# A state-space, attention and expert block on one core: joint projection of an order's two directions, a third of a convolution on VectorE, the value bias outside TensorE, routing of the last image by halves

## The chip, the cores and the metric

The kernel runs on one core of a Trainium2 chip. The metric is the device time of one execution in microseconds (us), a median of several runs. A core has TensorE (PE, matrix products; PEld is its weight load), VectorE (DVE), ScalarE (ACT), GpSimd (POOL) and SyncE (SP), which here only issues DMAs. Each engine runs its own instructions in their written order, and semaphores order the engines among each other.

## What is computed

Four images of 32x32 pixels with 384 channels pass three residual layers. Shortened from the reference:

```python
x = x + L0(_gn(x))                       # state-space layer, 4 scans
t = _to_tokens(x)                        # 4096 tokens of 384
t = t + L1_attn(_ln_t(t))                # linear attention, 12 heads
t = t + L1_ffn(_ln_t(t))                 # 8 experts, top 1, capacity 512

# L0
xz = x @ in_proj_w.T
xh, z = jnp.split(xz, 2, axis=-1)        # 192 channels each
xc = silu(depthwise_conv3x3(xh) + conv_b)
xs = [by rows, by columns, by rows flipped, by columns flipped]      # K = 4
x_dbl = jnp.einsum('bkdl,kcd->bkcl', xs, x_proj_w)
dts, Bs, Cs = jnp.split(x_dbl, [R, R + N], axis=2)                   # R = 24, N = 16
dts = softplus(jnp.einsum('bkrl,kdr->bkdl', dts, dt_projs_w) + dt_projs_b)
out_y = selective_scan(xs, dts, -exp(A_logs), Bs, Cs, Ds)
y = norm(sum of the four orders) * silu(z);  return y @ out_proj_w.T

# L1_attn, without softmax
attn = jnp.einsum('bhnd,bhmd->bhnm', q, k) / sqrt(32)
out = jnp.einsum('bhnm,bhmd->bhnd', attn, v);  return out @ w_proj + b_proj

# L1_ffn
expert_gate, expert_index = max and argmax of softmax(xf @ router_w)
position_in_expert = running count of the tokens of that expert      # dropped from 512 on
h = gelu(expert_inputs @ w1 + b1);  y = gelu(h @ w2 + b2);  out = gate * y
```

## The kernel before

**Layout.** All of it is one program with six stages; every SBUF tile is a view of one tensor, `arena`, and every PSUM tile a view of `ps`, so the profile's rows are told apart by their lines. Two images lie above each other on the 128 partitions (a pair, `p` = 0 or 1), each with 64 of the 192 channels, so the channels make J = 3 thirds of a pair. A direction `k` = 0 to 3 is an order `o = k % 2` (rows, columns) and a sense `dr = k // 2` (forward, flipped). An order's two directions have the same input.

**Prologue (0 to 258 us).** Group norm, input projection `in_proj` (L1048), the 3x3 convolution and the preparation of the scans. Pair 0's convolution and the first third of pair 1's are nine taps each on VectorE (`taps` L1486, `first_third` L1498 and L1502). The second and third thirds of pair 1 are on PE: seven taps as products with diagonal matrices (`conv`, 14 matmuls a third in two calls, L1060), the last two on VectorE (`last_taps`, L1517). The order is written out by tables: `FILL_ORDER` gives the two PSUM slots in turn, `CONV_AT` the half after whose `delta_product` a call of `conv` stands, `LAST_TAPS_AT` the same for VectorE, `SILU_AT` the step at which ScalarE applies silu to pair 1.

After the convolution each pair has HALVES = 12 halves: direction `k` by third `j`, `(k, j) = divmod(i, J)`. For each direction `x_proj(p, k)` (6 matmuls, L1076) puts the time-step rows on PSUM partitions 0 to 47 and the rows of B and C on 64 to 127. ScalarE copies them out (`split_hi`: L713 for the rows that later work reads, L714 for the bf16 high part); VectorE subtracts that (`split_rest`, L1530), ScalarE casts the middle part (`split_mid`, L718), VectorE subtracts again (`split_lo`, L1534). So B and C are kept as three bf16 parts that the scans' PE products add up. SP stores them in HBM (`store_parts`). Each half then takes these steps, and each engine runs them one half after another:

- PE: `delta_product` (2 matmuls, L1088); the line shows 4 instructions, as fp32 matmuls count twice in the trace.
- ScalarE: `dt_out` (absolute value L729, plain copy L730), `exp_abs` (L735), for even halves `one_more` (1 + u, L744), and for the half before `log_w` (L749).
- VectorE: for odd halves 1 + u itself (L1546), then `lost_part` (L1549), and for the half before `finish` (L1556, L1559, L1563).
- SP: `store_delta`, two stores a half. The buffers of a half turn over MADE = 4 places, those of 1 + u over 2, which is why a step waits for `pd_ok` of two halves before.

GpSimd copies pair 1's convolved thirds into column order (`by_columns`, L552) in between.

**Scans (258 to 1414 us).** 12 tiles of 32 units on PE, ScalarE, VectorE (L1628, L1645) and GpSimd (L564, L581). The change doesn't touch them.

**Norm, gate, output projection (1414 to 1504 us), then attention (1504 to 1708 us).** Per image: `mirror`, `keys` (one row of sums L1302, then L1307), `values` (L1316 and, for the bias of the values, one matmul a third with one row of contraction, L1318), `mixed` (L1325), `bias_row` (L1331), `weights` (L1345), `attend` for eight tiles (L1356), with the next image's `turn_and_gram` (L1279 to L1287) put in between. VectorE takes `keys`, `values` and `bias_row` out of PSUM (L1771, L1775, L1781, L1788) and adds the result to the tokens (`attended`, L1795, L1796).

**Routing.** Per image VectorE runs `stats`, `rsqrt`, `normalise`, `logits`, `choose`, `place` (L1802 to L1873), with an exp on ScalarE and two small products on PE (`cumsum`, L1337, L1338) between. GpSimd then scatters the image's 8 tiles of tokens to their slots in HBM (`scatter`, L619). Images 0 to 2 do this during the next image's attention. For image 3 nothing follows: all eight tiles are attended, then routed, then scattered; SP loads the second weights of expert 0 (L511) as soon as the slots are known, and after the last scatter the slots of expert 0 (L514) and the weights of expert 1 (L516, L517). **Experts (1741 to 2258 us):** `turn_slots` (L1393), then w1 (L1404) and w2 (L1416); an expert starts when both of its weights are in.

## Time and profile before

| | |
|---|---|
| median of 3 runs | 2261.23 us (2260.4 to 2262.72) |
| the profiled execution, its own time | 2259.55 us |
| its span in the trace | 2257.7 us |
| busy: PE / VectorE / GpSimd / ScalarE | 88% / 70% / 58% / 51% |
| TensorE clock granted, mean | 0.971 |

The span is what the trace covers, and 1.85 us of the execution lie around it. A page of the profile gives the busy share of each engine in 40 slices, the chain of waits that ended last, and the instructions in groups by line. Busy shares are means over stages with different limits, so each stage is read on its own. In a row, "[5.15 <-ACT arena L744]" means that the engine stood idle for 5.15 us before it, and that the instruction of line 744 on ScalarE ended this.

### The profile page before, as it was taken

The page shows a single profiled execution, that of the slowest core. Times are in us where ns is not written, and L with a number is a line of the kernel's source. Part 1 is how long each engine was busy: PE and PEld are TensorE (multiplying, and loading weights), DVE is VectorE, ACT ScalarE, POOL GpSimd, SP SyncE. Part 2 cuts the span into 40 slices and gives each one's busy share as a digit, 9 for nine tenths or more (in the row PEclk, how much of TensorE's full clock was granted, in tenths as well). Part 3 has the DMA queues.
Part 4 walks back from the last instruction along what each step waited for, and adds up shares of the span by engine and source line. Part 5 has one row for each costly group of instructions (what it writes and reads, how often), then busy time and mean ns, then how long its engine had stood idle before and what let it go on. Part 6 is the DMA issues. An engine that isn't in the chain of part 4 may idle for free.

```text
span 2257.7 us, 20191 instructions
## 1 busy us (share of the span) xinstructions
PE 1996.3 (88%) x5862; PEld 923.9 (41%) x5862; DVE 1579.7 (70%) x1480; ACT 1150.4 (51%) x1249; POOL 1299.1 (58%) x464
## 2 busy tenths in 40 slices
PE   7998588888888888888888888989994999999997
PEld 3433133333333333333333333456652555555554
DVE  6899999999999999999999999753553000000000
ACT  4789676767666676766666776211221121111111
POOL 0110399999999999999999999401333011111110
PEclk9996599999999999999999999999997999999999
DMA  5447622133222233222232220511226133333300
GB/s 187 178 162 265 209 75 75 57 107 83 78 70 65 74 102 88 65 74 74 71 96 70 79 65 19 228 42 56 84 85 237 64 121 124 124 119 125 126 24 7
DMA packets 79346, 228.84 MB, mean 101 GB/s; under 512 B 10895, under 2 KB 37121, under 8 KB 77760
## 3 DMA queue, kind: packets, MB, share of 16 engines
q1 hardware_dynamic: 73152, 211.25, 29.1%
q0 software_dynamic: 6144, 16.98, 2.1%
q8 instruction: 24, 0.39, 0.1%
q14 instruction: 26, 0.21, 0.0%
HBM read 166.10 MB, written 64.03 MB: 102 GB/s over the span
## 4 chain that ended last, share of the span: by engine, by line
PE 44%; DVE 26%; issue 17%; POOL 9%; ACT 3%; DMA 1%; DVEq 0%; ACTq 0%; POOLq 0%; SPq 0%
DVE arena L1645 15%; PE ps L1404 11%; PE ps L1416 11%; PE ps L1147 6%; POOL arena L581 5%; POOL arena L564 4%; PE ps L1356 3%; PE ps L1131 2%; DVE arena L1486 2%; DVE ps L1628 1%; PE ps L1144 1%; PE ps L1307 1%; PE ps L1048 1%; PE ps L1345 1%; DVE arena L1556 1%
## 5 line engine op out<-in xcount | busy, mean ns | idle before, releaser
L581 POOL TENSOR_TENSOR arena<-arena 128x2048 f32<-128x2048 f32 x192 | 871.3, 4551 | 17.6 <-DVE arena L1645 16.6
L1147 PE MATMUL ps<-arena 128*128 128x512 f32 x1536 | 726.5, 595 | 29.0 <-POOL arena L581 28.9
L1645 DVE TENSOR_TENSOR_SCAN arena<-arena,ps 128x1024 f32<-128x1024 f32 x264 | 588.9, 2276 | 0.0
L844 ACT ACTIVATE arena<-ps 128x1024 f32<-128x1024 f32 x384 | 390.7, 1017 | 249.0 <-PE ps L1131 247.1
L1131 PE MATMUL ps<-arena 96*128 (+1 forms) x1296 | 366.6, 384 | 128.1 <-DVE arena L1645 112.9
L1147 PEld LDWEIGHTS ps<-arena 128*128 128x128 f32 x1536 | 287.8, 189 | 288.6 <-issue 192.9
L564 POOL TENSOR_TENSOR arena<-arena 128x1024 f32<-128x1024 f32 x120 | 283.9, 2366 | 94.3 <-DMA arena<-b_rows 94.3
L1943 DVE TENSOR_TENSOR arena<-ps,arena 128x384 f32<-128x384 f32 x32 | 17.8, 558 | 449.7 <-PE ps L1416 449.7
L1628 DVE TENSOR_TENSOR ps<-ps,arena 128x1024 f32<-128x1024 f32 x264 | 310.1, 1223 | 13.2 <-PE ps L1131 13.2
L837 ACT ACTIVATE arena<-arena 128x1024 f32<-128x1024 f32 x264 | 300.7, 1139 | 9.0 <-DVE arena L1645 8.6
L1131 PEld LDWEIGHTS ps<-arena 96*128 96x128 bf16 x1296 | 112.8, 98 | 460.2 <-DVE arena L1645 216.3
L641 POOL DMA_INDIRECT out<-arena x32 | 31.7, 992 | 436.6 <-DVE arena L1948 436.6
L1645 DVE TENSOR_TENSOR_SCAN arena<-ps,arena 128x1024 f32<-128x1024 f32 x120 | 272.8, 2273 | 4.6 <-ACT ps L837 4.2
L1416 PE MATMUL ps<-arena 128*128 128x384 f32 x768 | 250.2, 486 | 0.0
L1404 PE MATMUL ps<-arena 128*128 128x512 f32 x576 | 249.5, 594 | 0.0
L1416 PEld LDWEIGHTS ps<-arena 128*128 128x128 f32 x768 | 145.4, 190 | 101.6 <-issue 3.8
L837 ACT ACTIVATE ps<-arena 128x1024 f32<-128x1024 f32 x120 | 134.1, 1118 | 87.5 <-DVE arena L1645 87.5
L1404 PEld LDWEIGHTS ps<-arena 128*128 128x128 f32 x576 | 109.9, 191 | 136.3 <-issue 134.0
L981 ACT ACTIVATE arena<-ps,arena 128x512 f32<-128x512 f32 x96 | 66.0, 688 | 176.0 <-PE ps L1404 175.9
L614 POOL TENSOR_TENSOR arena<-arena 128x384 f32<-128x384 f32 x32 | 27.0, 874 | 190.7 <-DVE arena L1788 190.7
L988 ACT ACTIVATE arena<-arena 128x384 f32<-128x384 f32 x32 | 16.7, 523 | 232.3 <-DVE arena L1943 232.3
L552 POOL COPY arena<-arena 128x1024 f32<-128x1024 f32 x6 | 14.6, 2454 | 145.7 <-ACT arena L702 145.7
(211 smaller groups left out, 1632.6 us busy)
## 6 DMA issues: line engine op xcount, KB each, us to landing
arena<-b_rows SPq DMA_DIRECT2D x240, 256.0 KB, 4.2
arena<-in_w SPq DMA_DIRECT2D x16, 2304.0 KB, 16.3
delta<-arena SPq DMA_DIRECT2D x24, 512.0 KB, 2.7
delta_x<-arena SPq DMA_DIRECT2D x24, 512.0 KB, 2.7
arena<-delta SPq DMA_DIRECT2D x24, 512.0 KB, 3.6
arena<-delta_x SPq DMA_DIRECT2D x24, 512.0 KB, 4.6
slot_in<-arena SPq DMA_DIRECT2D x8, 772.0 KB, 8.1
arena<-slot_in SPq DMA_DIRECT2D x8, 772.0 KB, 18.0
```

Source lines behind the costliest of these rows:

```text
L564: nc.gpsimd.tensor_tensor(xin[:, x % XRING], xin[:, x % XRING], dux[:, dr], ALU.mult).then_inc(in_ok, 1)
L581: nc.gpsimd.tensor_tensor(hst[:, h:h + 2], hst[:, h:h + 2], c_sb[:, c:c + 2], ALU.mult).then_inc(p2_ok, 2)
L837: nc.scalar.activation(dst, dlt[:, dr], ACT.Exp, scale=a_neg[:, q % OJ, dr, n:n + 1]).then_inc(dec_ok, 1)
L844: nc.scalar.activation(c_sb[:, u % RING], C_PS, ACT.Copy).then_inc(c_free, 1)
L981: nc.scalar.activation(h_sb[:, m], ps[:, 3 + m % 3, :], ACT.Gelu_apprx_tanh, bias=b1_col[:, e, m:m + 1]).then_inc(hg_ok, 1)
L1131: mm = pe.matmul(dst[:, h * 512:(h + 1) * 512], sel_lhs[0:BR, n], bc[0:BR, q % OJ // J, dr, m, h * 512:(h + 1) * 512], start=True, stop=True)
L1147: mm = pe.matmul(Y_PS[:, h * 512:(h + 1) * 512], ident, hst[:, u % HRING, h * 512:(h + 1) * 512], start=False, stop=(u == UN - 1))
L1356: mm = pe.matmul(ps[:, attend_bank(i), 0:CA], xnT[:, b % 2, t, i * P:(i + 1) * P], w_eff[:, t], start=(t == 0), stop=(t == CT - 1))
L1404: mm = pe.matmul(ps[:, 3 + m % 3, :], w1[s][:, t, m * P:(m + 1) * P], xeT[:, s, t], start=(t == 0), stop=(t == CT - 1))
L1416: mm = pe.matmul(ps[:, 6 + i % 2, 0:C], h_sb[:, m, i * P:(i + 1) * P], w2[s][:, m], start=(m == 0), stop=(m == MT - 1))
L1628: nc.vector.tensor_tensor(x, x, dux[:, dr], ALU.mult).then_inc(p1_ok, 1)
L1645: nc.vector.tensor_tensor_scan(h, f, x, 0.0, ALU.mult, ALU.add).then_inc(sc_ok, 1)
```

## The change

It has five parts.

1. **Joint projection.** `x_proj` is now called for an order: once for the time-step rows of both directions ("xd", 64 partitions each) and once for B and C of both ("xa"), 6 matmuls each, so 8 calls in all as before. ScalarE copies the time-step rows (`dt_rows_out`); for "xa" it copies the rows (`split_hi`, first) and casts the high part from all 128 partitions (second). PE subtracts the high part inside PSUM with `minus` (a negated identity in bf16, `take_hi`), ScalarE casts the middle part (`split_mid`), PE subtracts it (`take_mid`), ScalarE casts the low part (`split_lo`). VectorE has no part in it. The four directions come in the order `K_ORDER` = 0, 2, 1, 3. The weights of the projection are loaded by four DMAs in pieces of 64 floats, the weights `dt_w` a second time for the partitions from 64 on.
2. **Convolution.** VectorE convolves the second third of pair 1 as well, with nine taps; PE keeps the third one. VectorE makes 1 + u for two halves of three (`i % J`) instead of one of two, ScalarE for the other.
3. **Bias of the values.** The three products with one row are gone. `keys` puts its row of sums on all 128 partitions; VectorE scales it by the bias as a column (`bv_col`) and adds it before the mask.
4. **Routing of the last image by halves.** Four tiles each (`ROUTED`): statistics per tile as it is attended, the first half's slots and scatter before the second half's. ScalarE normalises the last image's tokens (two ACTIVATEs a tile) and takes the inverse root as exp(-0.5 ln).
5. **Expert 0's second weights** have a semaphore of their own, are loaded after the slots, and PE waits for them between w1 and w2.

```diff
+ROUTED = [(b, 0, TB) for b in range(B - 1)] + [(B - 1, 0, TB // 2), (B - 1, TB // 2, TB)]
...
-FILL_ORDER.insert(len(IN_ORDER) - 1, ("x", 0, 0))
-FILL_ORDER += [("x", 0, 1), ("conv", 1, 1), ("x", 0, 2), ("x", 0, 3), ("conv", 1, 2)]
-FILL_ORDER += [("x", 1, k) for k in range(K)]
+FILL_ORDER.insert(len(IN_ORDER) - 1, ("xd", 0, 0))
+FILL_ORDER += [("xa", 0, 0), ("xd", 0, 1), ("conv", 1, 2), ("xa", 0, 1)]
+FILL_ORDER += [("xd", 1, 0), ("xa", 1, 0), ("xd", 1, 1), ("xa", 1, 1)]
...
-CONV_AT = {1: (1, 0), 4: (1, 1), 7: (2, 0), 8: (2, 1)}
-LAST_TAPS_AT = {4: 1, 8: 2}
-SILU_AT, NEXT_PAIR_AT = HALVES - 3, HALVES - 2
+CONV_AT = {3: 0, 4: 1}
+LAST_TAPS_AT = 5
+SILU_AT = 6
+DT_ROWS_AT = {(0, 2): (0, 1), (0, 8): (1, 0), (1, 1): (1, 1)}
+BC_ROWS_AT = {(0, 0): (0, 0), (0, 5): (0, 1), (0, 10): (1, 0), (1, 3): (1, 1)}
+HI_AT = {(0, 0): (0, 0), (0, 6): (0, 1), (1, 0): (1, 0), (1, 4): (1, 1)}
+K_ORDER = (0, 2, 1, 3)
...
+            for k in range(K):
+                o, dr = k % 2, k // 2
+                sp.dma_start(xproj_w[:, o, :, :, H2 * dr:H2 * dr + H2],
+                             a["xproj_w"][:, k].rearrange("p j (s c) -> p j s c", s=2)).then_inc(ld_c, 16)
...
-            sp.wait_ge(idx_ok, B)
-            sp.dma_start(w2[0], w2_v[0]).then_inc(ld_w[0], 16)
+            sp.wait_ge(idx_ok, B + 1)
             sp.wait_ge(scat, 16 * NT)
             slot_in_v = slot_in.rearrange("(e i p) c -> e p i c", i=CPT, p=P)
             sp.dma_start(xe, slot_in_v[0]).then_inc(ld_xe, 16)
+            sp.dma_start(w2[0], w2_v[0]).then_inc(ld_w2[0], 16)
...
+                nc.scalar.activation(b_full[0:H2 + SR], slot[0:H2 + SR], ACT.Copy).then_inc(hi_ok, 1)
+                nc.scalar.activation(parts[:, o, 0], slot, ACT.Copy).then_inc(hi_ok, 1)
+
+            def split_mid(p, o):
+                act.wait_ge(less_ok, 2 * (p * 2 + o) + 1)
+                nc.scalar.activation(parts[:, o, 1], fill_slot("xa", p, o), ACT.Copy).then_inc(mid_ok, 1)
...
                     if s < HALVES:
                         dt_out(p, s)
                         exp_abs(p, s)
-                        if s % 2 == 0:
+                        if s % J == 0:
                             one_more(p, s)
                     if s >= 1:
                         log_w(p, s - 1)
...
+                    if (p, s) in HI_AT:
+                        split_hi(*HI_AT[p, s])
+                    if (p, s - 1) in HI_AT:
+                        split_mid(*HI_AT[p, s - 1])
+                    if (p, s - 2) in HI_AT:
+                        split_lo(*HI_AT[p, s - 2])
+                    if (p, s - 1) in DT_ROWS_AT:
+                        dt_rows_out(*DT_ROWS_AT[p, s - 1])
...
+            def take_part(p, o, part):
+
+                for h in range(2):
+                    mm = pe.matmul(fill_slot("xa", p, o)[:, h * 512:(h + 1) * 512], minus, parts[:, o, part, h * 512:(h + 1) * 512],
+                                   start=False, stop=True, skip_group_check=True)
+                return mm
...
                     if s + 1 < HALVES:
                         delta_product(p, s + 1)
...
+                    if (p, s - 2) in HI_AT:
+                        take_mid(*HI_AT[p, s - 2])
                     if p == 0 and s in CONV_AT:
...
+                    if (p, s - 1) in HI_AT:
+                        take_hi(*HI_AT[p, s - 1])
+                    if (p, s) in BC_ROWS_AT:
+                        x_proj("xa", *BC_ROWS_AT[p, s])
+                    if (p, s) in DT_ROWS_AT:
+                        x_proj("xd", *DT_ROWS_AT[p, s])
...
-                    mm = pe.matmul(ps[:, VK_PS, t * P:(t + 1) * P], bkv[0:1, 1, t * P:(t + 1) * P], w_row[0:1, t * P:(t + 1) * P],
-                                   start=False, stop=True, skip_group_check=True)
...
+            chain.link(nc.vector.tensor_tensor(by_block, bv_rows, ident.unsqueeze(1).to_broadcast([P, CT, P]), ALU.mult))
+            chain.link(nc.vector.tensor_reduce(bv_col, by_block, AX.X, ALU.add))
...
-                nc.vector.tensor_tensor(bd.rearrange("p t c -> p (t c)"), ps[:, VK_PS, 0:C], head_mask, ALU.mult).then_inc(bd_ok, 1)
+                if b:
+                    dve.wait_ge(m_ok, b * CT)
+                flat = bd.rearrange("p t c -> p (t c)")
+                chain.link(nc.vector.tensor_tensor(flat, ps[:, VK_PS, 0:C], w_row, ALU.add))
+                nc.vector.tensor_tensor(flat, flat, head_mask, ALU.mult).then_inc(bd_ok, 1)
...
+            for i in range(1, 4):
+                attended(b, i)
+                tile_stats(b, i - 1)
+            tile_stats(b, 3)
+            last_means(0)
+            attended(b, 4)
+            tile_stats(b, 4)
+            logits(b)
+            attended(b, 5)
+            choose(b)
+            attended(b, 6)
+            tile_stats(b, 5)
+            gates(b)
+            attended(b, 7)
+            tile_stats(b, 6)
+            tile_stats(b, 7)
+            last_means(1)
+            place(b)
+            logits(b + 1)
+            choose(b + 1)
+            gates(b + 1)
+            place(b + 1)
```

How the tables move PE's work in the middle of pair 0 is seen best in its instructions. Before, from the second call of `conv` (L1060) on, with `delta_product` (L1088) and `x_proj` (L1076) between:

```order
L1060 MATMUL ps<-arena 128x512 x7
L1088 MATMUL ps<-arena 128x512 x4
L1076 MATMUL ps<-arena 128x512 x6
L1088 MATMUL ps<-arena 128x512 x2
L1060 MATMUL ps<-arena 128x512 x7
L1088 MATMUL ps<-arena 128x512 x2
L1060 MATMUL ps<-arena 128x512 x7
```

and now the same stretch, `conv` on L1123, `delta_product` on L1167, `x_proj` on L1139, the subtraction of a part on L1147:

```order
L1147 MATMUL ps<-arena 128x512 x2
L1139 MATMUL ps<-arena 128x512 x6
L1167 MATMUL ps<-arena 128x512 x2
L1123 MATMUL ps<-arena 128x512 x7
L1167 MATMUL ps<-arena 128x512 x2
L1123 MATMUL ps<-arena 128x512 x7
L1167 MATMUL ps<-arena 128x512 x2
L1139 MATMUL ps<-arena 128x512 x6
```

Two calls of `conv` are gone. The other two stand directly behind an "xd" projection and ahead of an "xa" projection, with one `delta_product` between each (those of halves 4, 5 and 6).

ScalarE now, at half 6 of pair 0 (`dt_out` L767 and L768, `exp_abs` L773, `one_more` L782, `log_w` L787, `split_hi` L747 and L748, silu L729):

```order
L773 ACTIVATE arena<-arena 128x1024
L782 ACTIVATE arena<-arena 128x1024
L787 ACTIVATE arena<-arena 128x1024
L747 ACTIVATE arena<-ps 96x1024
L748 ACTIVATE arena<-ps 128x1024
L843 ACT_TABLE_LOAD
L729 ACTIVATE arena<-arena 128x1024 x3
L846 ACT_TABLE_LOAD
L767 ACTIVATE arena<-ps,arena 128x1024
```

The silu stood at step 9, between two halves and with no copies ahead of it; it is at step 6 now, right behind a `one_more` and the two copies of a `split_hi`.

VectorE at the end of the last image's routing, from the last `attended` on (before, everything from the statistics to `place` stood behind it):

```order
L1871 TENSOR_TENSOR arena<-arena,ps 128x384
L1895 BN_STATS arena<-arena 128x6 x2
L1902 BN_AGGR arena<-arena 128x2 x4
L1904 TENSOR_SCALAR arena<-arena 128x4
L1956 TENSOR_TENSOR arena<-ps,arena 128x32
...
L1976 TENSOR_TENSOR arena<-arena 128x4
L1919 TENSOR_TENSOR arena<-arena 128x4
...
L1936 TENSOR_TENSOR arena<-arena 128x32
L1942 TENSOR_REDUCE arena<-arena 128x4
...
L1976 TENSOR_TENSOR arena<-arena 128x4
```

Behind the last tile now come `place` of the first half (L1956 to L1976, which releases its scatter), then `logits`, `choose`, `gates` and `place` of the second half; the first half's `logits`, `choose` and `gates` have moved ahead, between the tiles.

## Rows read from the trace of the kernel before

**Rows 1.** By stage: length; busy PE, PEld, DVE, ACT, POOL; PE clock; DMA; GB/s.

```profile
92.00:158.00 66.00, 64.44 (x141) 25.73 (x140) 57.47 (x50) 60.01 (x59) 0.00 (x0) 0.97 0.45 160
158.00:258.00 100.00, 70.36 (x109) 25.01 (x107) 96.38 (x82) 84.85 (x85) 7.26 (x3) 0.64 0.63 224
...
1708.00:1741.00 33.00, 4.17 (x18) 3.73 (x18) 12.06 (x51) 3.03 (x5) 9.13 (x10) 0.56 0.76 265
```

**Rows 2.** VectorE in time order, 80 to 258 us: start, duration, idle before.

```profile
101.47 1.23 DVE L1549 SCALAR_TENSOR_TENSOR arena<-arena 128x1024 f32<-128x1024 f32 x1 [5.15 <-ACT arena L744]
...
160.94 2.83 DVE L1549 SCALAR_TENSOR_TENSOR arena<-arena 128x1024 f32<-128x1024 f32 x1
...
202.23 1.23 DVE L1549 SCALAR_TENSOR_TENSOR arena<-arena 128x1024 f32<-128x1024 f32 x1
...
207.03 1.22 DVE L1549 SCALAR_TENSOR_TENSOR arena<-arena 128x1024 f32<-128x1024 f32 x1
```

**Rows 3.** VectorE by line, 80 to 258 us: busy, mean ns, idle before.

```profile
L1502 DVE SCALAR_TENSOR_TENSOR arena<-arena 128x1024 f32<-128x1024 f32 x8 | 11.9, 1487 | 0.3
L1530 DVE TENSOR_TENSOR arena<-ps,arena 64x1024 f32<-64x1024 f32 x8 | 9.8, 1228 | 0.2
L1534 DVE TENSOR_TENSOR arena<-arena 64x1024 bf16<-64x1024 f32 x8 | 9.8, 1222 | 0.3
L1546 DVE TENSOR_SCALAR arena<-arena 128x1024 f32<-128x1024 f32 x12 | 9.1, 757 | 1.9 <-ACT arena L735 1.7
L1517 DVE SCALAR_TENSOR_TENSOR ps<-arena,ps 128x1024 f32<-128x1024 f32 x2 | 2.6, 1290 | 0.1
```

**Rows 4.** ScalarE in time order: the same step of two halves in a row.

```profile
113.60 1.11 ACT L729 ACTIVATE arena<-ps,arena 128x1024 f32<-128x1024 f32 x1
...
117.50 1.11 ACT L729 ACTIVATE arena<-ps,arena 128x1024 f32<-128x1024 f32 x1
```

**Rows 5.** ScalarE by line, 92 to 258 us: a table load.

```profile
L803 ACT ACT_TABLE_LOAD x1 | 1.3, 1283 | 0.0
```

**Rows 6.** PE in time order, prologue: products and their time at either clock.

```profile
96.35 5.42 PE L1076 MATMUL ps<-arena 128*128 128x512 f32 x12
...
103.61 6.28 PE L1060 MATMUL ps<-arena 128*128 128x512 f32 x14
109.81 3.70 PE L1088 MATMUL ps<-arena 48*128 48x512 f32 x8
...
173.73 7.19 PE L1088 MATMUL ps<-arena 48*128 48x512 f32 x8 [7.82 <-ACT arena L713]
180.85 8.09 PE L1076 MATMUL ps<-arena 128*128 128x512 f32 x12
```

**Rows 7.** DMA traffic from 20 to 22 us.

```profile
DMA packets 1177, 0.60 MB, mean 298 GB/s; under 512 B 760, under 2 KB 1142, under 8 KB 1155
```

**Rows 8.** PE in time order, `values` and `mixed` of image 3.

```profile
1676.11 0.48 PE L1318 MATMUL ps<-arena 1*128 1x128 f32 x2
1676.53 0.94 PE L1316 MATMUL ps<-arena 128*128 128x128 f32 x6
...
1679.81 2.24 PE L1325 MATMUL ps<-arena 128*128 128x392 f32 x6 [0.65 <-DVE arena L1781]
```

**Rows 9.** VectorE in time order, image 3's last tile and routing.

```profile
1708.41 0.55 DVE L1796 TENSOR_TENSOR arena<-arena,ps 128x384 f32<-128x384 f32 x1
...
1717.46 0.22 DVE L1850 TENSOR_TENSOR arena<-ps,arena 128x64 f32<-128x64 f32 x1
...
1721.08 0.17 DVE L1873 TENSOR_TENSOR arena<-arena 128x8 uint32<-128x8 f32 x1
```

**Rows 10.** GpSimd in time order, the first of image 3's eight scatters.

```profile
1722.05 0.97 POOL L619 DMA_INDIRECT slot_in<-arena  x1 [16.77 <-DVE arena L1873]
```

**Rows 11.** The chain that ended last, from the last scatter on.

```profile
1730.99 2.49 DMA slot_in<-arena
1733.50 4.59 DMA arena<-slot_in
```

More of the change, by code:

```diff
@@ L429, in _ @@
             for p in range(NP):
-                store_parts(p, 0)
                 if p == 0:
@@ L628, in _ @@
             scatter(B - 1)
+            scatter(B)
             def residuals(e, s):
@@ L1835, in choose, with tile_stats, last_means @@
-            def choose(b):
-                tb = slice(b * TB, (b + 1) * TB)
+            def tile_stats(b, i):
+                dve.wait_ge(ta2_ok, 1 + b * TB + (i + 1))
+                ins = nc.vector.bn_stats(bst5[:, i], tok[:, b * TB + i, :])
+                if i % 4 == 3:
+                    chain.link(ins)
+            def last_means(g):
+                settled(dve)
+                for i in range(4 * g, 4 * g + 4):
+                    ins = nc.vector.bn_aggr(mv5[:, i], bst5[:, i])
+                chain.link(ins)
+                nc.vector.tensor_scalar(neg_mean[:, 4 * g:4 * g + 4], mv5[:, 4 * g:4 * g + 4, 0], -1.0, None, ALU.mult).then_inc(tvar_ok, 1)
```

414 lines of the change are left out of this document (228 added, 186 removed).

## Prediction

> **What bounds the kernel now.** I first split the span by stage [rows 1], since the change touches three stages and leaves the scans and the experts alone.
>
> From 158 to 258 us VectorE is busy for 96.4 of 100 us, ScalarE for 84.9, PE for 70.4 at a granted clock of 0.64. So VectorE sets the end of the prologue, and ScalarE is close behind. From 92 to 158 us it is less clear: VectorE 57.5 of 66, ScalarE 60.0, PE 64.4 at full clock. In time order [rows 2] VectorE has one large hole, 5.15 us before its first `lost_part` at 101.47, where it waits for ScalarE. Later two halves in a row start 4.80 us apart (202.23 and 207.03): that is VectorE's price of a half without 1 + u. ScalarE's is 3.90 us (113.60 to 117.50, [rows 4]), one of its `one_more` or copies adds 1.0 to 1.1.
>
> Image 3's routing (1708 to 1741 us) is a stretch in which PE works for 4.2 of 33 us [rows 1]: a plain chain of VectorE, GpSimd and DMA. Attention before it is PE's.
>
> **The change, part by part.**
>
> *Prologue, VectorE's sum.* L1530 and L1534 go: 16 instructions of 1.23 us, 1.26 with the gap [rows 3], -20.1 us. Two last taps of 1.29 go, -2.6. L1546 grows from 12 to 16, 4 x 0.73 = +2.9. The third on VectorE is one TENSOR_SCALAR of 0.76 and eight taps of 1.3 (the mean of 1.49 in [rows 3] holds one that GpSimd's copy slowed), +11.2. Sum -8.6 us. But 11.2 - 2.5 of this lies before 101.47, where there is a hole of 5.15: VectorE comes to its first `lost_part` at 105.0, 3.5 later. From there on it has 17.3 us less to do. If VectorE stayed the only bound, the prologue would end 13.8 us earlier.
>
> *Prologue, what is late next.* It won't stay so. I lay the three engines' instructions in their new order, each as long as in the rows, each behind what it waits for. The same laying out of the old order gives the three holes of before up to 0.3 us and the end up to 2.2. Four places open:
>
> - Start: ScalarE's two copies of `split_hi` wait for "xa", which PE ends at 92.8 + 2 x 1.8 + 5.3 = 101.7 [rows 6]. Half 1's exp ends at 107; VectorE waits 0.9 us.
> - Halves 5 to 7, the largest. PE's `take_mid` waits for ScalarE until 109, behind it the "xd" projection ends at 115.2, `delta_product` 117.0, `conv` 6.2 (125.0 with the next product), `conv` again, product of half 6 at 133.0. ScalarE wanted it at 129.0. From 133.1 it has half 6 with `one_more` and the log of half 5 (5.3), the two copies (2.1), two table loads of 1.28 [rows 5] with three silus of 1.1 between (5.9), half 7 up to its exp (3.0): 149.4. VectorE is done at 142.4: a hole of 7.1 us, after one of 0.7. Before, the silu stood at half 9, where VectorE was behind and had no hole.
> - Second pair: 1.9 us behind the copies of "xa" (1, 0), 3.9 us at half 15, where ScalarE's `split_lo` waits 2.8 for `take_mid`, which stands behind an "xd" projection at half clock; 0.7 us at half 18.
>
> New holes 15.2 us, old ones after 101.47 some 2.3 in that laying out, so +13. Against it: GpSimd's three column copies slow VectorE's instructions that run beside them (2.83 us for one that takes 1.23 otherwise, [rows 2]), and they now fall mostly into the hole of 7.1 us, -3. Sum: +3.5 - 17.3 + 13 - 3 = **-4 us**, bounds -14 (all holes covered) and +2 (each of them half as long again). I take -4.5 for the term, since the trace has a further hole of 1.5 us at 195 that the laid out order hasn't.
>
> *PE in the prologue.* Eight projections stay. `conv` loses 14 matmuls of 6.28 in two calls, 12.6 us; eight pairs of bf16 products come, under 1 us a pair. PE isn't the bound except in the place above.
>
> *The weights of the projection.* They arrive in 3072 pieces of 256 bytes. In 2 us at 20 to 22 us the queues moved 760 packets under 512 bytes beside others [rows 7]: 3072 are 8.1 us, behind traffic that ends at 28. VectorE first asks for them at 38.5, so I cost this at nothing; bounds 0 and +4 (landing at 43 instead of 36). 
>
> *Attention.* L1318 goes: three per image, 0.42 us from its start to the next one's [rows 8], 12 in all, -5.1. PE has no hole there, so it counts in full. The second instruction of `values_out` (about 0.5) hides behind `turn_and_gram` (2 us) for images 0 to 2; for image 3 PE waits 0.65 for it [rows 8], so +0.6. `keys` loads 128 columns of weights instead of one, +0.1 an image. The column of the bias (two instructions of 0.5, before the tokens of tile 4 are normed, where PE waits for VectorE) +1.0. Sum **-3.1**, bounds -4.5 and -1.
>
> *Routing of image 3.* Before: last tile added at 1708.96, slots at 1721.25, eight scatters 1.28 apart from 1722.05 to 1730.99 [rows 9, 10], landing 2.5, slots in 4.6 [rows 11]. Now VectorE ends that tile at some 1709.5 (statistics between the tiles), two tiles' statistics 1.0, means 0.6, `place` of the first half 2.7 (L1850 to L1873 took 3.8 with the gates, [rows 9]), so its four scatters run from 1714.7 to 1719.8 beside VectorE's second half: logits 1.4, choose 1.1, gates 0.6, the cumulative sum's way over PE 0.7, place 2.7, slots at 1720.3. That is only 1 us earlier than before, but four scatters are left, not eight: 4 x 1.28 = 5.1. Sum **-6.0**. ScalarE's 16 ACTIVATEs of some 0.5 us and its two inverse roots end before the slots do. Bounds -8 (the slots' load, no longer behind 2.3 MB of weights) and -2 (ScalarE's tokens late).
>
> *Expert 0's weights.* They are asked for some 6 us later than before, behind the slots, and needed only after the expert's 36 products with w1, which take most of half an expert: nothing.
>
> **Sum:** -4.5 - 3.1 - 6.0 = -13.6 us. The profiled execution took 2259.55 us; on its own time that is 2246.0, against the median, which is 1.7 higher, **2247.6 us**.
>
> **The rivals.**
>
> *VectorE stays the bound in the prologue.* For it: it was the busiest for 100 us, and it starts pair 0 with work in hand. Against: ScalarE has 24 x 3.9 [rows 4] + 8 x 1.1 for `one_more` + 19 copies of 1.03 + 5.9 for silu = 128 us of work for the same 24 halves, so hardly any slack. -14 in place of -4.5: 2238.
>
> *The halves bring little.* If the last image's tokens, normalised on ScalarE, or the exp behind them come late, the second scatter starts late. Against it: 8 us of ScalarE work have 11 us. -2 in place of -6: 2251.6.
>
> *Slower: PE at half clock on the path.* PE has less to do and waits for ScalarE's casts in its own order. After 7.82 us of waiting the clock was at half and a projection took 8.09 us for 5.42 [rows 6]. If all eight projections lay on the path at that clock, 8 x 2.7 = 21.5 us come: 2269. It decides from five of eight on (13.6 / 2.7). Against it: only one or two have somebody waiting behind them.
>
> *The change does what it says* in all of its parts, as the listed instructions show; a part that adds nothing is in the range.
>
> **How the numbers follow.** The forecast 0.68, VectorE as the only bound 0.13, little from the halves 0.12, the slower case 0.04, several terms at their small ends together 0.03. The range reaches from a prologue of -11 to terms of -1.5, -1.5 and -4: **2240 to 2254**. A measurement of this kernel tells 0.2%, 4.5 us, from no change. Faster by more than that 0.93, same 0.03, slower 0.04.
>
> **What would show it.** VectorE's last `finish` near 253 instead of 257.7 us, with a hole of about 7 us in it near 145, ended by ScalarE. No instruction between 75 and 258 us on VectorE on 64 partitions. An attention image 1.2 us shorter. Four scatters from about 10 us before the other four, slots loaded some 6 us earlier after the last tile. It would be wrong if VectorE showed no hole in the prologue (gain too small), if PE stood at half clock with ScalarE waiting for it in most halves (too large), or if the last scatter came as long after the last tile as before.

## The result, and the profile after

| | before | after |
|---|---|---|
| median of the first runs (4 each) | 2261.47 us (2260.4 to 2262.72) | 2245.59 us (2243.82 to 2246.91) |
| the profiled execution, its span | 2259.55, 2257.7 us | 2246.46, 2244.7 us |
| ratio of the runs, 95% interval | | 0.9929 (0.9912 to 0.9946) |
| TensorE clock granted, mean | 0.971 | 0.968 |

The change makes the kernel 15.9 us faster; 2247.6 was forecast. The two profiled executions differ by only 13.0 us of span. The other 2.7 us lie in the profile of before that was taken first (the second one, below, shows it).

VectorE of the changed kernel in the prologue, and ScalarE beside it in the middle of pair 0, in order of time:

```profile
103.99 1.22 DVE L1621 SCALAR_TENSOR_TENSOR arena<-arena 128x1024 f32<-128x1024 f32 x1
107.45 0.69 DVE L1618 TENSOR_SCALAR arena<-arena 128x1024 f32<-128x1024 f32 x1 [2.25 <-ACT arena L773]
...
131.97 0.69 DVE L1618 TENSOR_SCALAR arena<-arena 128x1024 f32<-128x1024 f32 x1 [2.51 <-ACT arena L773]
...
153.21 0.69 DVE L1618 TENSOR_SCALAR arena<-arena 128x1024 f32<-128x1024 f32 x1 [7.07 <-ACT arena L773]
...
200.00 1.22 DVE L1621 SCALAR_TENSOR_TENSOR arena<-arena 128x1024 f32<-128x1024 f32 x1 [2.14 <-ACT arena L782]
...
253.46 2.36 DVE L1688 TENSOR_TENSOR ps<-ps,arena 128x1024 f32<-128x1024 f32 x2
```

```profile
128.87 1.11 ACT L767 ACTIVATE arena<-ps,arena 128x1024 f32<-128x1024 f32 x1 [4.11 <-PE ps L1167]
...
136.99 1.11 ACT L767 ACTIVATE arena<-ps,arena 128x1024 f32<-128x1024 f32 x1 [4.11 <-PE ps L1167]
...
144.28 1.28 ACT L843 ACT_TABLE_LOAD   x1
145.58 3.23 ACT L729 ACTIVATE arena<-arena 128x1024 f32<-128x1024 f32 x3
148.82 1.28 ACT L846 ACT_TABLE_LOAD   x1
```

The first `lost_part` (L1621) starts at 103.99 us, 2.5 later than before [rows 2], the scans (L1688) at 253.46, 4.3 earlier than the 257.75 of before. Between these two, VectorE before and after (columns as in [rows 1]):

```profile
101.47:257.75 156.28, 125.33 (x227) 47.12 (x226) 149.38 (x127) 136.35 (x135) 7.26 (x3) 0.76 0.57 204
```

```profile
103.99:253.46 149.47, 115.47 (x207) 41.48 (x210) 127.67 (x116) 125.97 (x128) 5.68 (x3) 0.73 0.61 216
```

VectorE works 21.7 us less (149.38 to 127.67) and stands idle 14.9 us more (6.9 to 21.8). So +2.5 - 21.7 + 14.9 = -4.3.

Image 3's routing, VectorE and GpSimd in order of time, against [rows 9, 10]:

```profile
1701.29 0.54 DVE L1871 TENSOR_TENSOR arena<-arena,ps 128x384 f32<-128x384 f32 x1
...
1706.06 0.16 DVE L1976 TENSOR_TENSOR arena<-arena 128x4 uint32<-128x4 f32 x1
...
1712.51 0.16 DVE L1976 TENSOR_TENSOR arena<-arena 128x4 uint32<-128x4 f32 x1
```

```profile
1707.02 0.97 POOL L645 DMA_INDIRECT slot_in<-arena  x1 [8.84 <-ACT arena L981]
...
1713.47 0.97 POOL L645 DMA_INDIRECT slot_in<-arena  x1 [1.64 <-DVE arena L1976]
...
1717.30 0.97 POOL L645 DMA_INDIRECT slot_in<-arena  x1 [0.30 <-issue]
```

The last tile is added at 1701.29, the last slots are out 11.2 us later (12.7 before) and the last scatter starts 16.0 us later (22.6 before).

### The profile page after: what moved, and what is told of

The parts are those of the page before. It is cut to its first block, busy times and chain, and to the rows that moved or that the text cites. A ratio compares the mean times of both kernels' runs of the same rounds, so it can differ in the third digit from the quotient of the medians.

```text
span 2244.7 us, 20167 instructions
## 1 busy us (share of the span) xinstructions
PE 1984.1 (88%) x5826; PEld 919.6 (41%) x5830; DVE 1575.2 (70%) x1505; ACT 1144.9 (51%) x1258; POOL 1297.0 (58%) x464
## 3 DMA queue, kind: packets, MB, share of 16 engines
q1 hardware_dynamic: 76208, 211.54, 29.6%
## 4 chain that ended last, share of the span: by engine, by line
PE 46%; DVE 23%; issue 17%; POOL 8%; ACT 3%; DMA 1%; DVEq 0%; SPq 0%; ACTq 0%; POOLq 0%
DVE arena L1705 15%; PE ps L1489 11%; PE ps L1502 11%; PE ps L1229 6%; POOL arena L604 4%; POOL arena L587 4%; PE ps L1439 3%; PE ps L1213 2%; PE ps L1110 2%; DVE ps L1688 1%; PE ps L1226 1%; PE ps L1139 1%; PE ps L1390 1%; PE ps L1428 1%; DVE arena L1572 1%
## 5 line engine op out<-in xcount | busy, mean ns | idle before, releaser
L604 POOL TENSOR_TENSOR arena<-arena 128x2048 f32<-128x2048 f32 x192 | 868.3, 4533 | 16.6 <-DVE arena L1705 15.7
L1688 DVE TENSOR_TENSOR ps<-ps,arena 128x1024 f32<-128x1024 f32 x264 | 309.1, 1216 | 12.6 <-PE ps L1213 12.6
L1489 PEld LDWEIGHTS ps<-arena 128*128 128x128 f32 x576 | 110.1, 191 | 136.8 <-issue 134.4
```

The lines of the kernel that those rows point to most:

```text
L604: nc.gpsimd.tensor_tensor(hst[:, h:h + 2], hst[:, h:h + 2], c_sb[:, c:c + 2], ALU.mult).then_inc(p2_ok, 2)
L1489: mm = pe.matmul(ps[:, 3 + m % 3, :], w1[s][:, t, m * P:(m + 1) * P], xeT[:, s, t], start=(t == 0), stop=(t == CT - 1))
L1688: nc.vector.tensor_tensor(x, x, dux[:, dr], ALU.mult).then_inc(p1_ok, 1)
```

## The experiments

All are variants of the changed kernel but one; each is named with the median of its runs and its ratio to the kernel before, measured on the same chip. The changed kernel's 0.9929 is 2245.6 us. The 95% interval of a ratio is some 3 us wide to either side, so the times alone don't tell the silu one half later, the weights in whole pieces, all of 1 + u on VectorE, the second weights first or the sums ahead from the changed kernel. There the verdict rests on the stage in the trace, and each says which.

### The kernel before, profiled again

> The kernel before, unchanged, profiled once more. In the first profile VectorE's three sums of the first orders (L1669) at the end of the scans took 3.02 us while GpSimd's last product beside them took 7.16; in every profile of the changed kernel and its variants the same three took 8.55 to 8.56 and the product 5.18. Theory A (chance: who is served first there differs from run to run, and the profiled run of before was a lucky one): the three sums may take some 8.5 us here, and then the span is 1.5 to 3 us longer, 2259 to 2261 us. Theory B (the two kernels differ there in every run): 3.0 us again, span within 1 us of 2257.7.

Ratio 0.9998 (0.9988 to 1.0008), span 2260.4 us. The sums of the first orders (L1669; L1670 here; L1729 after) on VectorE and GpSimd's last product beside them (L581; L582; L604), first profile of before, second profile, and after:

```profile
1414.00 3.02 DVE L1669 TENSOR_TENSOR arena<-arena 128x512 f32<-128x512 f32 x3
1414.24 7.16 POOL L581 TENSOR_TENSOR arena<-arena 128x2048 f32<-128x2048 f32 x1 [0.45 <-DVE arena L1645]
```

```profile
1413.40 8.56 DVE L1670 TENSOR_TENSOR arena<-arena 128x512 f32<-128x512 f32 x3
1413.62 5.19 POOL L582 TENSOR_TENSOR arena<-arena 128x2048 f32<-128x2048 f32 x1 [0.44 <-DVE arena L1646]
```

```profile
1409.02 8.55 DVE L1729 TENSOR_TENSOR arena<-arena 128x512 f32<-128x512 f32 x3
1409.23 5.18 POOL L604 TENSOR_TENSOR arena<-arena 128x2048 f32<-128x2048 f32 x1 [0.42 <-DVE arena L1705]
```

Theory A holds: the first profile was a lucky one, and a rare one, since no other run of before on record is as short as its 2259.55 us (the lowest is 2260.03). From these sums to image 0's first turn it is 76.40 us in the first profile (1414.00 to 1490.40) and 79.86 in the second (1413.40 to 1493.26). So the stages are better compared with the second, whose span is 15.7 us longer than that of after, which fits the medians. Its marks, then those of after, each in order of time on PE, with VectorE's last tile between: image 0's first turn, `mirror`, the last tile, the slots turned.

```profile
1493.26 0.55 PE L1280 MATMUL ps<-arena 128*128 128x128 f32 x3
...
1508.72 0.30 PE L1297 MATMUL ps<-arena 128*128 128x128 f32 x1 [1.12 <-ACT arena L907]
...
1711.27 0.55 DVE L1797 TENSOR_TENSOR arena<-arena,ps 128x384 f32<-128x384 f32 x1
...
1740.89 2.79 PE L1394 MATMUL ps<-arena 128*128 128x128 f32 x12 [20.86 <-DMA arena<-slot_in]
```

```profile
1488.68 0.55 PE L1361 MATMUL ps<-arena 128*128 128x128 f32 x3
...
1505.26 0.30 PE L1378 MATMUL ps<-arena 128*128 128x128 f32 x1 [1.12 <-ACT arena L942]
...
1724.43 2.79 PE L1478 MATMUL ps<-arena 128*128 128x128 f32 x12 [14.70 <-DMA arena<-slot_in]
```

| stage, up to | before (second profile) | after | the stage's own share |
|---|---|---|---|
| the scans' start | 257.25 | 253.46 | -3.8 |
| image 0's first turn | 1493.26 | 1488.68 | -0.8 |
| `mirror` of image 0 | 1508.72 | 1505.26 | +1.1 |
| the last tile added | 1711.27 | 1701.29 | -6.5 |
| slots turned | 1740.89 | 1724.43 | -6.5 |
| the end | 2260.4 | 2244.7 | +0.8 |

How well a stage repeats says how much its share is worth. From `mirror` of image 0 to the last tile it is 202.55 us in both profiles of before, 196.03 after, and 196.02 to 196.05 in nine of the ten other profiles that leave this stage alone (196.38 in one). From the last tile to the slots turned it is 29.6 to 29.8 before and 23.06 to 23.24 in all profiles with this routing and this order of loads. The scans' start, the way from there to the first turn, and the experts move by 1 to 3 us between executions of one and the same code, so the shares of -0.8 (to the first turn) and +0.8 (the end) say nothing of the change.

### The changed kernel, once more

> The changed kernel, unchanged, once more. In its first profile and in five of the variants PE's first projection of B and C (at 95 us) took 7.0 to 7.1 us, with the granted clock at 0.50 from 96 to 98 us; in four others, whose code is the same up to there, 5.42 us at full clock. Theory A (this differs from execution to execution, and the end of the prologue with it): either 5.42 us and a prologue that ends at 251 to 252 us, or 7.1 and 253 to 254; the median of the runs 2244 to 2247 us. Theory B (the differing code behind decides it): 7.1 us and 253.5 us again, and the silu one half later then really gained 2 us.

2244.61 us (2243.92 to 2248.98), ratio 0.9931 (0.9917 to 0.9944). PE's first "xa" and its next "xd" projection (L1139; L1140 and L1137 in the variants) in three executions of the same prologue: after, after once more, and the variant with the weights in whole pieces, whose projections do the same work.

```profile
95.43 7.08 PE L1139 MATMUL ps<-arena 128*128 128x512 f32 x12
...
111.13 7.67 PE L1139 MATMUL ps<-arena 128*128 128x512 f32 x12
```

```profile
95.16 7.11 PE L1140 MATMUL ps<-arena 128*128 128x512 f32 x12
...
110.89 6.00 PE L1140 MATMUL ps<-arena 128*128 128x512 f32 x12
```

```profile
95.35 5.42 PE L1137 MATMUL ps<-arena 128*128 128x512 f32 x12
...
108.42 7.48 PE L1137 MATMUL ps<-arena 128*128 128x512 f32 x12
```

Neither theory as written: the first was 7.11 us again and the prologue ended at 251.74. Eight profiles with this prologue fall into three groups by the two durations: 7.1 and 7.7 end at 253.5 (two), 7.1 and 6.0 to 6.1 at 251.5 to 251.8 (three), 5.4 and 7.5 to 7.6 at 250.8 to 251.4 (three, the silu one half later among them). So the end of the prologue goes by 1 to 3 us with where PE's clock stands at half in an execution, and a single profile tells no smaller step. For the change itself this means that the second profile puts the scans' start 5.5 to 6.0 us earlier than before (251.74 against 257.25 and 257.75), the first 3.8 to 4.3.

### The silu one half later

> The silu of pair 1 with its two table loads stands one half later on ScalarE (step 7 in place of 6); nothing else changes. In the changed kernel VectorE has its largest hole, 7.07 us, at 153.2. Theory A (the place of the silu makes the hole, and the hole is a loss of its own): the hole at 153 shrinks to 1 to 2 us, the one at the next half stays under 2, and the prologue ends 4 to 6 us earlier, 2240 to 2242 us. Theory B (ScalarE's order of work carries the end, and a hole on VectorE is only the other face of it): the hole splits in two, some 1 and 4 us, the holes after 185 us grow by what is gained, and the end comes 0 to 1.5 us earlier, 2244 to 2246 us.

```diff
-SILU_AT = 6
+SILU_AT = 7
```

2244.04 us, ratio 0.9929 (0.9915 to 0.9942). The hole at 153 became 1.20 us, one of 3.37 opened a half later, and the scans start at 251.23, as in the other executions with the same two projections (250.75 and 251.38). Theory B: moving the silu alone moves the hole.

### The tables one half later

> Only the tables of the prologue change: the second call of conv stands one half later, with its last taps, the silu, the second order's B and C projection and the three steps of its split; in pair 1 the second order's two projections and its split also stand one half later. Same instructions, same number. Theory A (the 13 us of new holes are the order's, not the work's: PE held ScalarE 4.11 us twice behind conv and the split's wait at 192 us): ScalarE's two waits of 4.11 us fall under 2 each, VectorE's holes after 104 us sum to some 12 us in place of 19, the prologue ends 4 to 7 us earlier, 2239 to 2242 us. Theory B (ScalarE's sum of work sets the end, the order moves only where VectorE waits): the sum of the holes stays within 2 us, 2244 to 2247 us.

```diff
-CONV_AT = {3: 0, 4: 1}
-LAST_TAPS_AT = 5
-SILU_AT = 6
+CONV_AT = {3: 0, 5: 1}
+LAST_TAPS_AT = 6
+SILU_AT = 7
-DT_ROWS_AT = {(0, 2): (0, 1), (0, 8): (1, 0), (1, 1): (1, 1)}
-BC_ROWS_AT = {(0, 0): (0, 0), (0, 5): (0, 1), (0, 10): (1, 0), (1, 3): (1, 1)}
-HI_AT = {(0, 0): (0, 0), (0, 6): (0, 1), (1, 0): (1, 0), (1, 4): (1, 1)}
+DT_ROWS_AT = {(0, 2): (0, 1), (0, 8): (1, 0), (1, 2): (1, 1)}
+BC_ROWS_AT = {(0, 0): (0, 0), (0, 6): (0, 1), (0, 10): (1, 0), (1, 4): (1, 1)}
+HI_AT = {(0, 0): (0, 0), (0, 7): (0, 1), (1, 0): (1, 0), (1, 5): (1, 1)}
```

SP's `store_parts` of the second order follows by one half too. 2240.79 us (2239.14 to 2242.89), ratio 0.9908 (0.9893 to 0.9923). VectorE between its first `lost_part` and the scans:

```profile
104.85:246.12 141.27, 114.84 (x208) 41.13 (x208) 132.36 (x116) 123.78 (x126) 8.72 (x3) 0.72 0.64 229
```

Idle 8.9 us in place of 21.8, and the scans start at 246.12, 5 us earlier than in executions with the same two projections. The holes shrank by 12.9 us, but VectorE's busy time grew by 4.7 (127.67 to 132.36) for the same instructions: in the changed kernel GpSimd's three copies ran in the hole of 7.07 us (5.68 us), here they run beside VectorE's work (8.72 us), and instructions of VectorE beside them take longer, one 2.82 us for 1.22. ScalarE's wait of 4.11 behind the first call of `conv` is still there (at 127.3); the second is gone. From 195 us on VectorE has no hole. Theory A: the holes came from the order, several places at once. With most of them closed VectorE is busy for 132.4 of 141.3 us and is the nearest to being the bound again; that it is, no run with this order tests.

### VectorE makes all of 1 + u

> VectorE makes 1 + u in all halves; ScalarE's eight instructions of 1.06 us for it are gone, VectorE gets eight of 0.70. Theory A (in the changed kernel ScalarE is the bound of the prologue): its end comes 4 to 8 us earlier, 2238 to 2242 us. Theory B (neither engine is the bound by its sum; they hand the path to each other and to PE, and what one gives up the other takes): within 1 us, 2244.5 to 2246.5 us. Theory C (VectorE is still the bound): 8 x 0.70 = 5.6 us later, 2250 to 2251 us.

```diff
-                        if s % J == 0:
-                            one_more(p, s)
...
-                if i % J:
-                    dve.wait_ge(u_ok, m + 1)
+                dve.wait_ge(u_ok, m + 1)
```

2247.03 us, ratio 0.9934 (0.9921 to 0.9948); the scans start at 254.24, against 253.46 in the execution with the same two projections. Theory B, though at its edge (its range ended at 2246.5): eight instructions less on ScalarE, eight more on VectorE, 0.8 us later. Neither engine's sum is the bound here.

### The second third on PE again

> The second third of pair 1 is convolved on PE again (14 products in two calls, the last two taps on VectorE), in the changed kernel; later steps of pair 0 stand one half later so that the slots of PSUM come out. Removed from VectorE: a third of 11.2 us, added two taps of 1.29 and seven builds of a diagonal of 0.19. Theory A (the third costs VectorE only what its hole ahead of pair 0 and the later holes cover, and PE with 12.6 us more would hold ScalarE instead): 0 to 6 us slower, 2246 to 2252 us, with ScalarE waiting for PE in halves 2 to 6. Theory B (VectorE's sum sets the end; the third was not free): 3 to 7 us faster, 2239 to 2243 us.

```diff
-FILL_ORDER += [("xa", 0, 0), ("xd", 0, 1), ("conv", 1, 2), ("xa", 0, 1)]
+FILL_ORDER += [("xa", 0, 0), ("conv", 1, 1), ("xd", 0, 1), ("conv", 1, 2), ("xa", 0, 1)]
...
-CONV_AT = {3: 0, 4: 1}
-LAST_TAPS_AT = 5
-SILU_AT = 6
-DT_ROWS_AT = {(0, 2): (0, 1), (0, 8): (1, 0), (1, 1): (1, 1)}
-BC_ROWS_AT = {(0, 0): (0, 0), (0, 5): (0, 1), (0, 10): (1, 0), (1, 3): (1, 1)}
-HI_AT = {(0, 0): (0, 0), (0, 6): (0, 1), (1, 0): (1, 0), (1, 4): (1, 1)}
+CONV_AT = {1: (1, 0), 2: (1, 1), 4: (2, 0), 5: (2, 1)}
+LAST_TAPS_AT = {3: 1, 6: 2}
+SILU_AT = 7
+DT_ROWS_AT = {(0, 3): (0, 1), (0, 8): (1, 0), (1, 1): (1, 1)}
+BC_ROWS_AT = {(0, 0): (0, 0), (0, 6): (0, 1), (0, 10): (1, 0), (1, 3): (1, 1)}
+HI_AT = {(0, 0): (0, 0), (0, 7): (0, 1), (1, 0): (1, 0), (1, 4): (1, 1)}
...
-            whole_third(1)
```

2250.44 us, ratio 0.9948 (0.9934 to 0.9962). VectorE in order of time:

```profile
99.60 1.23 DVE L1620 SCALAR_TENSOR_TENSOR arena<-arena 128x1024 f32<-128x1024 f32 x1 [6.77 <-ACT arena L782]
...
107.39 0.69 DVE L1617 TENSOR_SCALAR arena<-arena 128x1024 f32<-128x1024 f32 x1 [6.57 <-ACT arena L773]
...
161.13 0.69 DVE L1617 TENSOR_SCALAR arena<-arena 128x1024 f32<-128x1024 f32 x1 [7.08 <-ACT arena L773]
```

The scans start at 257.35, as late as before the change. The time that the third takes on VectorE was there for the taking, and ScalarE waits for PE's products of pair 0 for 0.89, 4.11 and 2.93 us (at 128.7, 136.8 and 144.9): theory A. Taking the parts off VectorE alone gave nothing in this order of work; whether another order would let it, and what the joint projection gives by itself, no run shows.

### The scatters behind all slots

> GpSimd's first four scatters of the last image wait for the slots of the second half too, so all eight run behind VectorE's last slots, as before the change; all else of the routing by halves stays. Theory A (the gain is that four scatters run beside VectorE): last scatter 4 x 1.28 = 5.1 us later less the 0.5 us by which the first starts at once, the gap from the last tile to the turned slots grows from 22.7 to some 27.5 us, 2250 to 2251 us. Theory B (the gain came from the shorter work on VectorE and ScalarE's share of it, the scatters are hidden anyway): under 1.5 us, 2245 to 2247 us.

```diff
-                pool.wait_ge(idx_ok, g + 1)
+                pool.wait_ge(idx_ok, B + 1 if b == B - 1 else g + 1)
```

2250.59 us, ratio 0.9950 (0.9937 to 0.9964), the last two scatter rows of GpSimd:

```profile
1720.86 0.97 POOL L645 DMA_INDIRECT slot_in<-arena  x1 [0.30 <-issue]
1722.13 0.97 POOL L645 DMA_INDIRECT slot_in<-arena  x1 [0.31 <-issue]
```

With the last tile at 1701.08 the last scatter starts 21.05 us behind it, 5.0 later than with the halves. Theory A.

### The bias on PE again

> The bias of the values is a product with one row of contraction on PE again, three an image, and its column, the row's scaling and the second instruction of the values on VectorE are gone. Theory A (each of the 12 products was 0.42 us on the path): attention from its first image to the last tile is 2.5 to 3.5 us longer, 2248 to 2249 us. Theory B (PE has holes behind VectorE and ScalarE at those places and takes the products in them): under 1 us, 2245 to 2247 us.

```diff
-                    mm = pe.matmul(ps[:, ROW_PS, 0:C], gram[:, t, C:C + 1].to_broadcast([P, P]), w_kv[:, t, 0:C],
+                    mm = pe.matmul(ps[0:1, ROW_PS, 0:C], gram[:, t, C:C + 1], w_kv[:, t, 0:C],
...
+                    mm = pe.matmul(ps[:, VK_PS, t * P:(t + 1) * P], bkv[0:1, 1, t * P:(t + 1) * P], w_row[0:1, t * P:(t + 1) * P],
+                                   start=(t == 0), stop=False, skip_group_check=True)
...
-            chain.link(nc.vector.tensor_tensor(by_block, bv_rows, ident.unsqueeze(1).to_broadcast([P, CT, P]), ALU.mult))
-            chain.link(nc.vector.tensor_reduce(bv_col, by_block, AX.X, ALU.add))
...
-                chain.link(nc.vector.tensor_tensor(flat, ps[:, VK_PS, 0:C], w_row, ALU.add))
-                nc.vector.tensor_tensor(flat, flat, head_mask, ALU.mult).then_inc(bd_ok, 1)
+                nc.vector.tensor_tensor(flat, ps[:, VK_PS, 0:C], head_mask, ALU.mult).then_inc(bd_ok, 1)
```

2250.54 us, ratio 0.9947 (0.9933 to 0.9961). `values` of image 0 in this variant, and in the changed kernel:

```profile
1513.86 0.48 PE L1397 MATMUL ps<-arena 1*128 1x128 f32 x2
1514.28 0.94 PE L1401 MATMUL ps<-arena 128*128 128x128 f32 x6
```

```profile
1514.99 2.17 PE L1399 MATMUL ps<-arena 128*128 128x128 f32 x18
```

Theory A in kind, but 5.6 us from image 0's first turn to the last tile (218.24 us here, 212.61 after), where 2.5 to 3.5 were expected. Three products with one row and the nine others (two instructions each, so x18) take 3.74 us from the first to the next `turn_and_gram` (1513.86 to 1517.60); the nine alone take 2.01 (1514.99 to 1517.00). So a product with one row costs 0.58 us: 0.42 until the next starts, and 0.16 by which three others behind it take longer than among their likes (0.77 to 0.87 us for 0.67). Why they do, no run shows. The column of the bias is gone here too, and the way from the first turn to `mirror` is 15.47 us, as before the change (15.46), where the changed kernel has 16.58.

### The weights in whole pieces

> The four loads of the projection's weights bring each direction's 128 floats in one piece (512 bytes) in place of two of 64 (256 bytes): half as many packets, the same bytes. The weights so land in wrong places, so the projection computes something else; its work is the same. Theory A (my forecast: the pieces cost nothing, the load lands before it is wanted): 0 to 0.3 us, and VectorE's wait for the constants is as long as before. Theory B (VectorE or ScalarE waited for the last piece at 37 to 44 us): VectorE's first tap at 44.4 us comes 1 to 4 us earlier and the whole with it, 2241 to 2244 us.

```diff
-                sp.dma_start(xproj_w[:, o, :, :, H2 * dr:H2 * dr + H2],
-                             a["xproj_w"][:, k].rearrange("p j (s c) -> p j s c", s=2)).then_inc(ld_c, 16)
+                sp.dma_start(xproj_w[:, k // 2, :, k % 2], a["xproj_w"][:, k]).then_inc(ld_c, 16)
```

2243.67 us, ratio 0.9927 (0.9914 to 0.9941). VectorE's first tap starts at 44.37 us, in the changed kernel at 44.45; theory A. The loads do differ: the DMA queues are busy until 30 us here (185 GB/s from 29 to 30, 8 from 30 to 31) and until 31 in the changed kernel (135 GB/s from 30 to 31, 0 behind). VectorE asks for the weights at 37.6.

### The second weights first

> Expert 0's second weights are asked for as soon as the first half's slots are known, ahead of the scatters' end and of the slots' load, as before the change (there at the slots of all). Theory A (the place of this load is worth nothing: it is through when the slots are loaded, or needed late): within 0.5 us, 2245 to 2246 us. Theory B (it takes the queues from the scatters or the slots): the scatters' last landing or the slots' load, 4.4 us now, grows by 1 to 4 us, 2246.5 to 2250 us.

```diff
+            sp.wait_ge(idx_ok, B)
+            sp.dma_start(w2[0], w2_v[0]).then_inc(ld_w2[0], 16)
             sp.wait_ge(idx_ok, B + 1)
             sp.wait_ge(scat, 16 * NT)
...
             sp.dma_start(xe, slot_in_v[0]).then_inc(ld_xe, 16)
-            sp.dma_start(w2[0], w2_v[0]).then_inc(ld_w2[0], 16)
```

2248.13 us, ratio 0.9940 (0.9927 to 0.9954). The chain that ended last, from the last scatter on, in the changed kernel and in this one:

```profile
1717.30 2.50 DMA slot_in<-arena
1719.86 4.43 DMA arena<-slot_in
```

```profile
1716.62 4.30 DMA slot_in<-arena
1720.99 4.41 DMA arena<-slot_in
```

Theory B. The weights are asked for at 1705.57, 11 us ahead of the last scatter, share the queues with the scatters (398 GB/s from 1712 to 1718 us, 100 in the changed kernel), and the last one lands 1.8 us later. So part 5 of the change keeps 1.8 us that routing by halves would otherwise lose. In the order of before it had nothing to keep: there the last scatter landed in 2.49 [rows 11], though the weights were asked for 9.7 us ahead of it (1721.28), since the stores of the last tokens were through by then (0 GB/s from 1720 to 1722). In the order of halves these stores still fill the queues until 1712 (352 GB/s from 1710 to 1712 in the changed kernel).

### The sums ahead of GpSimd's product

> In the changed kernel GpSimd's last product of the scans waits until VectorE has made the three sums of the first orders (for image 0's norm), so they no longer run beside each other; PE needs that product only behind the sums' own products. Theory A (the sums were held up by GpSimd's product, 8.55 us where 3.0 do): they take 3 us or less, PE's products of the mean come 4 to 5 us earlier, the input projection of image 1 some 2 to 3 us earlier, 2242.5 to 2244 us. Theory B (what stands behind, the projection's bias and GpSimd's later product, takes the gain): within 1 us, 2245 to 2247 us.

```diff
                     pool.wait_ge(sc_ok, U + 4)
+                    if last and u == UN - 2:
+                        pool.wait_ge(yt0_ok, J)
```

2243.05 us (2242.48 to 2244.32), ratio 0.9919 (0.9905 to 0.9932).

```profile
1407.98 2.99 DVE L1731 TENSOR_TENSOR arena<-arena 128x512 f32<-128x512 f32 x3
...
1411.20 4.52 POOL L606 TENSOR_TENSOR arena<-arena 128x2048 f32<-128x2048 f32 x1 [3.46 <-DVE arena L1731]
```

The sums take 2.99 us, the product alone 4.52. From PE's last long run of the scans to `mirror` of image 0 it is 97.5 us, in place of 100.1 and 100.7 in the two profiles of the changed kernel. Theory A.

### Both

> The tables of the prologue one half later, as before, together with GpSimd's last product behind VectorE's three sums. If the two gains lie in stages of their own they add: the prologue's end near 247 to 248 us, and 2237.5 to 2239.5 us in all. If the sums' gain is taken up behind them, 2240 to 2242 us.

2238.47 us (2233.91 to 2239.74), ratio 0.9899 (0.9884 to 0.9914), scans from 246.90. Its two projections took 7.08 and 7.67 us, as in the changed kernel's first profile, whose scans start at 253.46: against that execution the tables gain 6.6 us, the second time that they gain some 5 us or more. The gains add, to some 7 us under the changed kernel (whose second measurement has 0.9917 to 0.9944). It is the fastest version here.

## Why the prediction was right

The median came 2.0 us under the forecast of 2247.6, in the range. The sum of -13.6 us stood against -13.0 in the two spans it was made for, and part of that agreement is luck: the stage at the end of the scans was 3.5 us shorter in the first profile of before than in its second. Against the second profile the change gives -15.7. What the forecast left out is mostly attention, the one term that came out beyond its own bounds.

**Prologue, -4.5 forecast, -3.8 to -6.0 measured** (two executions of each kernel). In the first profile the main steps hold one by one. VectorE came to its first `lost_part` 2.5 us later (3.5 forecast), partly because all of the prologue was 0.9 us early from PE's first input projection on (6.95 us for 8.13), which no part of the change explains; the second profile of before has 7.70 there. It had 21.7 us less to do (17.3 and 3 for GpSimd's copies, forecast). The holes grew by 14.9 (13 forecast); the largest was 7.07 us, as laid out, ended by the exp of half 7. The small ones agree less well one by one (2.25 us for 0.9 at half 1, 2.51 and 1.18 at halves 5 and 6 for 0.7, 2.14 for 3.9 at half 15), so that their sum came out this near is partly luck. The holes of halves 5 to 7 were laid out some 4 us early: the products of halves 5 and 6 ended at 128.8 and 136.9 us, not 125.0 and 133.0, since PE stood at half clock in between: the second projection ahead of them took 7.67 us and the product in front of it 3.75 (106.62 to 110.30), and I had both at full clock, 5.42 and 1.98. The first projection's 7.08 us mattered less, as 0.9 us of it were in hand. That VectorE would not stay the bound is confirmed by its 21.8 idle us, and by the tables one half later: the same instructions in another order, and the scans start 5 us earlier. What I did not see is that those holes were mostly a matter of placing. "Hardly any slack" for ScalarE, in the first rival, was wrong: with the other tables it worked 123.8 of 141.3 us.

**Attention, -3.1 forecast, -5.4 measured** (+1.1 and -6.5), beyond its bound of -4.5. The bias column cost 1.1 us for 1.0, at the place named, and goes with it when it is taken out. The step that was off is the price of L1318: 0.42 us from its start to the next one's is not what goes with it. With the three gone the block of `values` is 1.73 us shorter (3.74 to 2.01), not 1.27, and the sum -6.9, not -5.1. The +0.6 of image 3 came (PE waits 1.31 us for VectorE ahead of `mixed`, where it waited 0.65), the +0.4 of `keys` did not: its first products take 2.10 us with 128 columns of weights as with one. That makes -6.3 of the -6.5; the rest is image 0, where it is 8.10 us from `mirror` to the next `turn_and_gram` in place of 8.38.

**Routing, -6.0 forecast, -6.5 measured.** Four scatters left, 5.1 by the forecast and 5.0 by the scatters held back; slots 1.5 us earlier for 1.0. One sentence of the forecast was wrong in itself: it had the first four scatters "about 10 us before the other four", though its own times give 6; it was 6.45.

**Expert 0's weights, 0 forecast.** Against the order of before, right. But the reason given, that they are needed late, was only half: left in front they would have cost 1.8 us. The stage behind is 0.8 us longer in the two profiles; w1's 36 products of expert 0 take 32.74 us in the first profile of after, 31.14 in its second, 32.05 in the second of before, so this is the moment at which the clock rises, not the change: from 1728 to 1730 us it was granted at 0.50 in the first profile of after and at 1.00 in its second, at slots turned 0.4 us apart.

**The pieces of 256 bytes, 0 forecast,** measured 0.1. The load itself was estimated too long: 8 us of load behind the traffic that ends at 28 would have landed at 36, and the queues were through at 31; pieces of 512 bytes saved 1 us of that.

**The rivals.** VectorE as the only bound and PE's clock as a loss of 20 us are out. Little from the halves is out by the scatters held back. The scans and the norm gave 0.8 us that I had not counted, within what two profiles differ by. How the prologue's gain divides between the joint projection and the third on VectorE stays open: the third was taken back alone, the projection never.

## What to carry to other kernels

When work is taken off the bounding engine, lay out the others' order at once and then move the table's entries together: one entry moved shifted a hole, eight moved closed most of them. Price a small product by the time of the whole block with and without it, not by its own distance to the next. And where the forecast is a sum against one profile, take a second profile of the same kernel: here two of them differed by 3.5 us in a stage that nobody had touched, while others repeated within 0.1 us.

## What the runs showed of the hardware that was not expected

- VectorE's sums of two SBUF tiles and GpSimd's product of two SBUF tiles, started 0.2 us apart, do not share evenly. VectorE starts first each time. In one execution of before VectorE's three took 3.02 us and GpSimd's product 7.16; in the second execution of before and in every one of the changed kernel 8.55 and 5.18 (to 0.01), the second of the three alone 5.33. Alone they take 2.99 and 4.52. The Trainium skill's page "SBUF — State Buffer" (section "SBUF: two separate sides") states that the port pair of the two is an exclusive lock which whoever starts first holds for the whole instruction; the durations agree with it. The case adds what becomes of three VectorE instructions in a row: its first had the pair each time (1.0 to 1.1 us), and behind it either VectorE's second went on (1.09 us) or GpSimd's product had its turn. That costs VectorE 5.5 us and the whole some 3. Two executions of one program went either way.
- TensorE's granted clock was at 0.50 (1.2 GHz) from 96 to 98 us in the changed kernel, though PE had worked without a gap before it; in the variant with whole pieces it was at 1.00 (2.4 GHz) in the same stretch. Of the twelve profiles with this stretch of code eight had 0.50 there and four 1.00. Clock is the third number from the end:

```profile
96.00:98.00 2.00, 2.00 (x3) 0.67 (x2) 1.93 (x3) 2.00 (x3) 0.00 (x0) 0.50 0.55 166
```

```profile
96.00:98.00 2.00, 2.00 (x6) 0.83 (x5) 1.93 (x3) 2.00 (x3) 0.00 (x0) 1.00 0.54 162
```

  It costs the projection 1.7 us when it comes. What brings it on no run here shows.
